# Encoder jobs of a hybrid transformer kernel: feed-forward, value products, norms and copies at other positions

## The reference

```python
x = x + encoder4(layernorm(x))   # 4 layers: 16 heads of 8, ALiBi + causal mask, FFN 128 -> 512 -> 128 with exact gelu, final norm
x = x + moe(layernorm(x))        # 8 experts, hyperbolic distances pick 2 of them per row
x = x + rope_attention(layernorm(x))
x = x + moe(layernorm(x))
```

## Time and profile before

| | us |
|---|---|
| median of 3 runs | 2651.41 (2651.28 to 2651.97) |
| profiled execution | 2659.2 |
| its span | 2657.4 |
| PE busy in the span | 2277.5 |
| DVE busy in the span | 1755.3 |
| ACT busy in the span | 1463.5 |

### The profile page before, as it was taken

The page is one execution under the profiler, slowest core; times in us unless marked ns, Lnnn a source line. Parts: engine busy times, 40 slices in busy tenths (PEclk is TensorE's granted clock), DMA queues, the critical chain, the costliest instruction groups (busy, mean ns, idle before and its releaser), DMA issues.

```text
span 2657.4 us, 102576 instructions
## 1 busy us (share of the span) xinstructions
PE 2277.5 (86%) x44398; PEld 1394.7 (52%) x44398; DVE 1755.3 (66%) x5525; ACT 1463.5 (55%) x2646; POOL 1037.8 (39%) x1261
## 2 busy tenths in 40 slices
PE   3689999999999999999998888996878778888983
PEld 1345555555555555555554444785644444436872
DVE  6877777777777777777877774422567777852212
ACT  0357677777677777777655556442245434454441
POOL 6334333333334333333444545423334554442135
PEclk9799999999999999999988988998888888889997
DMA  4253333342433333333222211575622222205773
GB/s 115 81 161 101 109 120 117 105 132 93 121 107 105 124 105 116 109 128 93 87 68 62 75 33 34 185 220 147 177 67 70 65 64 62 64 13 173 224 205 109
DMA packets 162531, 288.76 MB, mean 109 GB/s; under 512 B 28504, under 2 KB 116312, under 8 KB 160344
## 3 DMA queue, kind: packets, MB, share of 16 engines
q1 hardware_dynamic: 153696, 264.23, 33.0%
q0 software_dynamic: 8384, 17.97, 2.5%
HBM read 227.33 MB, written 95.96 MB: 122 GB/s over the span
## 4 chain that ended last, share of the span: by engine, by line
PE 61%; DVE 19%; ACT 7%; issue 4%; POOL 3%; SPq 2%; DMA 2%; another core or an unknown queue 2%; POOLq 0%; ACTq 0%; DVEq 0%
PE bank L481 23%; PE bank L647 9%; PE bank L601 9%; DVE mx L1281 6%; PE bank L787 5%; PE bank L797 5%; PE bank L665 3%; ACT big L878 3%; PE bank L488 2%; DVE xn L973 1%; DVE stats L960 1%; ACT OT L884 1%; PE bank L609 1%; ACT big L946 1%
## 5 line engine op out<-in xcount | busy, mean ns | idle before, releaser
L878 ACT ACTIVATE big<-bank 128x512 f32<-128x512 f32 x1600 | 919.8, 599 | 704.5 <-PE bank L481 662.5
L1281 DVE TENSOR_REDUCE mx<-bank 128x16 f32<-128x512 f32 (+1 forms) x1440 | 903.0, 654 | 417.1 <-PE bank L609 385.0
L1577 POOL TENSOR_SCALAR_AFFINE_SELECT big<-big 128x768 f32<-128x768 f32 (+1 forms) x640 | 392.9, 637 | 915.5 <-ACT big L878 915.1
L481 PE MATMUL bank<-QS,KS 99*32 99x512 bf16 (+3 forms) x10240 | 651.6, 312 | 46.1 <-ACT big L878 35.3
L601 PE MATMUL bank<-KS,QS 96*32 96x352 bf16 (+15 forms) x10240 | 592.5, 294 | 103.2 <-DVE mx L1281 63.4
L647 PE MATMUL bank<-big,V 128*9 128x512 f32 (+3 forms) x5120 | 457.8, 453 | 19.0 <-POOL big L1577 10.7
L601 PEld LDWEIGHTS bank<-KS,QS 96*32 96x32 bf16 x10240 | 243.1, 99 | 410.7 <-issue 177.3
L481 PEld LDWEIGHTS bank<-QS,KS 99*32 99x32 bf16 x10240 | 218.0, 99 | 220.4 <-ACT big L878 94.0
L609 PE MATMUL bank<-mask_a,ident_b 128*32 128x64 bf16 (+1 forms) x5760 | 305.8, 196 | 0.8 <-issue 0.5
L946 ACT ACTIVATE big<-bank,big 128x256 f32<-128x256 f32 x368 | 150.7, 471 | 253.4 <-PE bank L787 198.8
L647 PEld LDWEIGHTS bank<-big,V 128*9 128x9 f32 x5120 | 130.8, 92 | 154.7 <-issue 86.2
(11 more groups left out here) (216 smaller groups left out, 2727.4 us busy)
## 6 DMA issues: line engine op xcount, KB each, us to landing
big<-e_pack SPq DMA_DIRECT2D x92, 578.0 KB
QS<-part_scr SPq DMA_DIRECT2D x480, 96.0 KB
KS<-part_scr SPq DMA_DIRECT2D x480, 96.0 KB
part_scr<-parts SPq DMA_DIRECT2D x80, 384.0 KB
x_rows<-in_alibi SPq DMA_DIRECT2D x47, 384.0 KB, 4.9
y_rows<-in_alibi SPq DMA_DIRECT2D x47, 384.0 KB, 5.6
big<-x_rows SPq DMA_DIRECT2D x92, 128.0 KB
y_rows<-big SPq DMA_DIRECT2D x92, 128.0 KB
```

What stands on the lines that cost most here:

```text
L481: last = mm(out[c:c + 32], stationary[:, c:c + 32], moving, start=start, stop=stop)
L878: A(dst, src, ACT.Exp).then_inc(exp_done, 1)
L1281: v.tensor_reduce(mx[:, quad, k, 0:w], src, axis=AX.X, op=ALU.max).then_inc(a_used, 1)
L1577: g.affine_select(out=blocks, in_=blocks, compare_op=ALU.is_ge, fill=0.0, base=0, pattern=[[0, n], [1, P]], channel_multiplier=-1).then_in ...
```

## The change

Only positions change; no computation is added or left out. In encoder jobs the four positions without a maximum chunk are 13, 14, 22 and 38 instead of 9, 19, 29 and 39, so pass A of a job ends at position 29 instead of 28. The second feed-forward matrix goes in four pieces at positions 30, 30, 32 and 36. Rope jobs keep their positions. `TAIL_LEAD` is 6 instead of 5, and the late routing steps move by one position.

```diff
+WITHOUT = {False: (13, 14, 22, 38), True: (9, 19, 29, 39)}
-TAIL_LEAD, TAIL_RATE = 5, (2.0, 1.5)
+TAIL_LEAD, TAIL_RATE = 6, (2.0, 1.5)
 # PE, maximum chunks
-            quad, k = divmod(c, CPQ)
-            return (quad, k, APQ * quad + k) if k < APQ else (quad, None, None)
+            if (c - SKEW) % CHUNKS in WITHOUT[rope_job]:
+                return None, None, None
+            n = c - sum((pos + SKEW) % CHUNKS < c for pos in WITHOUT[rope_job])
+            return (*divmod(n, APQ), n)
 # PE
-                extras = [(xt, 2, (0, 1))]
+                extras = [(xt, 2, (0 if rope_job else 1, 1))]
-                    extras += [(lambda b, j, k=k: project(b, j, k), 2, (4 + 3 * k, 1)) for k in range(2)]
-                    extras += [(project_v, 2, (10, 1))]
+                    extras += [(lambda b, j, k=k: project(b, j, k), 2, (4 + 4 * k, 1)) for k in range(2)]
+                    extras += [(project_v, 2, (13, 1))]
-                    extras += [up_at(0, 26), up_at(1, 27), quad_at(1, (0,), 29), quad_at(1, (1,), 29),
-                               up_at(2, 29), up_at(3, 29), quad_at(1, (2, 3), 29)]
-                    extras += [(lambda b, j, t=t: ffn_down(b, j, t), -1, (29, 1)) for t in range(TT)]
+                KTS = ((0,), (1,), (2, 3))
+                if rope_job:
+                    quads = ((0, 0, (14, 18, 19)), (1, 0, (22, 23, 25)), (2, 0, (32, 33, 34)), (3, -1, (2, 3, 4)))
+                    sums = (7, 9, 11, 13)
+                else:
+                    quads = ((3, -1, (3, 5, 5)), (0, 0, (14, 19, 19)), (1, 0, (21, 29, 30)), (2, 0, (34, 38, 39)))
+                    sums = (7, 10, 12, 13)
+                if not rope_job:
+                    extras += [up_at(0, 28), up_at(1, 28), up_at(2, 29), up_at(3, 29)]
+                    extras += [down_at(0, 30), down_at(1, 30), down_at(2, 32), down_at(3, 36)]
-                extras += [(attn_transposes, -1, (15, 1)), (out_project, -1, (17, 1)), (max_transposes, 1, (31, 1))]
+                extras += [(attn_transposes, -1, (15 if rope_job else 16, 1)), (out_project, -1, (17 if rope_job else 18, 1)),
+                           (max_transposes, 1, (31 if rope_job else 33, 1))]
-                    extras += [(ffn_xt, -1, (24, 1))]
+                    extras += [(ffn_xt, -1, (25, 1))]
 # ACT: copy of xn 1 -> 2, of k 8 -> 9, sums of quads 0 to 2 20, 30, 36 -> 19, 31, 39, attention 15 -> 16
-                    extras += [(ffn_x, -1, (24, 1)), (ffn_gelu, -1, (27, 1))]
+                    extras += [(ffn_x, -1, (25, 1)), (ffn_gelu, -1, (27, 1))]
 # DVE
-                extras += [(add_x, -1, (18, 1)), (negate_split, 1, (28, 1)), (evac_max, 1, (31, 1)),
-                           (lns, 3, (33, 1)), (lna, 3, (36, 1))]
+                extras += [(add_x, -1, (18, 1)), (negate_split, 1, (28, 1) if rope_job else (30, 0)), (evac_max, 1, (31 if rope_job else 34, 1)),
+                           (lns, 3, (33 if rope_job else 25, 1)), (lna, 3, (36 if rope_job else 26, 1))]
-                    extras += [(ffn_lns, -1, (19, 1)), (ffn_lna, -1, (21, 1)), (ffn_add, -1, (30, 1))]
+                    extras += [(ffn_lns, -1, (19, 1)), (ffn_lna, -1, (21, 1)), (ffn_add, -1, (36, 1))]
 # POOL
-                          (lambda b, j: rsqrt(ln_index(b, j)), 3, (34, 1))]
+                          (lambda b, j: rsqrt(ln_index(b, j)), 3, (34 if rope_job else 26, 1))]
 # SP
-                          (lambda b, j: load(b, j, 1), 2, (20, 1)), (load_max, 1, (33 if rope_job else 32, 1)),
+                          (lambda b, j: load(b, j, 1), 2, (20, 1)), (load_max, 1, (33 if rope_job else 35, 1)),
```

More of the change, by code:

```diff
@@ L443, in spread_at @@
         def spread_at(n):
-            at = 23 if n == 0 else 24 + n if n <= 28 else 26 + n
+            at = 23 if n == 0 else 24 + n if n <= 28 else 27 + n
             return (-2 - at // CHUNKS, (at % CHUNKS, 1))
@@ L586, in pass_a @@
                 def pass_a(b, j, c):
-                    quad, k, n = a_chunk(c)
+                    quad, k, n = a_chunk(c, rope_job)
                     if k is None:
@@ L735, in attention @@
-                if not rope_job:
-                    extras += [up_at(0, 26), up_at(1, 27), quad_at(1, (0,), 29), quad_at(1, (1,), 29),
-                               up_at(2, 29), up_at(3, 29), quad_at(1, (2, 3), 29)]
-                    extras += [(lambda b, j, t=t: ffn_down(b, j, t), -1, (29, 1)) for t in range(TT)]
[L739 to L747, removed]
-                extras += [(attn_transposes, -1, (15, 1)), (out_project, -1, (17, 1)), (max_transposes, 1, (31, 1))]
+                def down_at(t, pos):
+                    return (lambda b, j: ffn_down(b, j, t), -1, (pos, 1))
@@ new lines, in quad_at @@
+                def quad_at(g, kts, rel, pos):
+                    return (lambda b, j: pv(b, j, g, kts), rel, (pos, 1))
+                KTS = ((0,), (1,), (2, 3))
[5 more added lines that the diff above has]
+                    sums = (7, 10, 12, 13)
@@ new lines, in attention @@
+                for g, rel, at in quads:
+                    extras += [quad_at(g, kts, rel, pos) for kts, pos in zip(KTS, at)]
+                if not rope_job:
+                    extras += [up_at(0, 28), up_at(1, 28), up_at(2, 29), up_at(3, 29)]
+                    extras += [down_at(0, 30), down_at(1, 30), down_at(2, 32), down_at(3, 36)]
+                extras += [(lambda b, j, t=t: ot_transposes(b, j, t), -1, (pos, 1)) for t, pos in enumerate(sums)]
+                extras += [(attn_transposes, -1, (15 if rope_job else 16, 1)), (out_project, -1, (17 if rope_job else 18, 1)),
+                           (max_transposes, 1, (31 if rope_job else 33, 1))]
@@ L755, in attention @@
                     route = ((route_transposes, 17), (route_project, 19), (route_dots, 22))
-                    extras += [(lambda b, j: route_ranks(j - ROUTE) if spread(j) else None, -3, (14, 1))]
+                    extras += [(lambda b, j: route_ranks(j - ROUTE) if spread(j) else None, -3, (15, 1))]
                     extras += [(lambda b, j, what=what: what(j - ROUTE) if j >= ROUTE else None, -2, (pos, 1))
@@ L888, in evac_attn @@
                     A(attnT[:], bankR[:], ACT.Copy).then_inc(attnT_ready, 1)
-                extras = [(xnt, 2, (1, 1))]
+                extras = [(xnt, 2, (1 if rope_job else 2, 1))]
                 if not rope_job:
[L892 to L896, removed]
+                    extras += [(lambda b, j, k=k: evac_qk(b, j, k), 2, (5 + 4 * k, 0)) for k in range(2)]
+                for g, rel, pos in ((3, -1, 5), (0, 0, 20 if rope_job else 19), (1, 0, 26 if rope_job else 31), (2, 0, 35 if rope_job else 39)):
+                    extras += [(lambda b, j, g=g: evac_ot(b, j, g), rel, (pos, 1))]
+                extras += [(evac_attn, -1, (15 if rope_job else 16, 1))]
                 def ffn_x(b, j):
@@ L1594, in attention @@
                     extras += [(lambda b, j: rsqrt(b + j, fln_step, frstd_ready), -1, (20, 1))]
-                    extras += [(lambda b, j, n=n: first_ln(b, j, n), 2, (17 + 8 * n, 1)) for n in range(2)]
+                    extras += [(lambda b, j, n=n: first_ln(b, j, n), 2, (17 + 6 * n, 1)) for n in range(2)]
                     route = ((lambda S: route_rsqrt(2 * S), -2, 1), (final_bias, -1, 33), (final_rows, -2, 4),
```

12 lines of the change are left out of this document (5 added, 7 removed).

## The result

The changed kernel takes 2708.89 us (median of 4 runs, 2706.53 to 2709.97); the kernel before, measured beside it, 2651.35 (2645.26 to 2651.97). The ratio is 1.0227, 95% interval 1.0207 to 1.0248: 57.5 us slower, where +36 were forecast and the range ended at 2704. The profiled execution took 2706.5 us, 47.3 more than that of before.

What follows compares the result with a forecast made beforehand. TensorE (PE), busy 86% of the span, was taken to bound the kernel, with its waits. 23 plain intervals x (0.7 waits + 0.9 clock) = +37 us on the median 2651.4 gave 2687 us, range 2625 to 2704.

Steps and rivals of the forecast that it cites:

- The main mechanism: Position 30's score chunk: PE waits 2.7 us a job for exp 28, its cover now standing behind the chunk.
- Chain on DVE: Output projection to second-layer transposes: the chain stays 6.0 us, PE has more work inside, gain 0.9 us a job.
- Load of the maxima: Position 0 of the next job: later copy and load make PE wait 0.5 us more, ends 0 and 1.5.
- DVE's wait for the power: Layer norm at 25 and 26: DVE waits about 0.7 us for POOL's square root; cost 0.2 us a job.
- The waits for maxima: PE's waits before the transposes and at positions 33 to 39 (0.67 us), expected to shrink or go.
- 45.7 + 0.7 = 46.4: Plain job without a clock fall: 45.7 us before, plus terms -0.9 + 2.7 - 1.8 + 0.2 + 0.5.
- other moves: Projections, head sums, attention transposes and positions without maximum chunk: 0 us a job, ends -0.4 and +0.4.
- The clock: PE's granted clock falls in 7 jobs of 10, 1.5 us each: +0.9 us a job, ends -0.2 and +1.3.
- The sum: 23 plain intervals x (0.7 + 0.9) = +37 us, routing jobs 0; added to median 2651.4, rounded down to 2687.
- The seven jobs with routing: Encoder jobs 25 to 31: 0 taken, as late DVE catches up in the wait; ends -20 and +15.
- Rival A: Faster: the 2.7 us wait overlaps with DVE lateness and DVE's relief stays; 2629 us, chance 0.27.
- Rival C: Worst: load of the maxima and layer norm at upper ends, a fall in every job; +2.6 x 23, 2711, chance 0.09.

Runs made afterwards that it cites:

- k2max_up: k2_max with the first up-projection at position 27 instead of 28; 2585.6 us, ratio 0.9773 to the kernel before.
- k2_slots: cover_k2 with the positions without a maximum chunk back at 9, 19, 29 and 39; 2632.1 us, ratio 0.9927 to the kernel before.
- k2_ln: cover_k2 with the layer norm back at 33 and 36 instead of 25 and 26, power on POOL at 34; 2685.1 us, ratio 1.0114.
- cover_k4: Changed kernel with the last value product and all four second-layer pieces at position 29; 2637.2 us, ratio 0.9952 to the kernel before.
- cover_k2: Changed kernel with the last value product and second-layer pieces 0 and 1 at 29, pieces 2 and 3 at 32 and 36; 2613.6 us, ratio 0.9859.
- after_max: Changed kernel with only the maxima's way earlier (transposes and copy at 32, load at 33), the wait for exp 28 left; 2689.3 us, ratio 1.017.
- k2_max: cover_k2 with the maxima's way earlier: transposes and DVE copy at 32, load on SP at 33; 2601.6 us, ratio 0.9809.
- before_apart: Kernel before with only the second-layer pieces at 30, 30, 32 and 36 instead of 29, the following addition at 36; 2678.6 us, ratio 1.0109.
- k2max_both: k2_max with the first up-projection at 27 and the pipeline-filling first layer norms moved earlier; 2584.7 us, ratio 0.9767 to the kernel before.
- cover_k: Changed kernel with only the last value product of quad 1 moved to position 29; 2654.7 us, ratio 1.0019 to the kernel before.

## Why the prediction was right and wrong

**The main mechanism was right, in place and size.** "PE waits 2.7 us in every job": 2.66 from start to start, 2.48 idle, 23 times in 23 jobs, released by exp 28. Chain on DVE: 5.75 us measured, 6.0 said. Load of the maxima: 0.45 us late, 0.5 said. DVE's wait for the power: 0.64 idle against 0.7. The waits for maxima are gone. A job without a fall takes 46.0 or 46.3, where 45.7 + 0.7 = 46.4 was worked out. Not costed was 0.29 us before the third up-projection, because the first gelu and its table load now start later with the first up-projection at 28; k2max_up later showed that this was worth 0.6 us a job.

**What took the waits for maxima away was put in the wrong place in part.** The longer one, ahead of the transposes, the prediction gave to the work that PE has more there, and said "6.0 us stay" for the chain; the free positions it put under "other moves", at 0 with ends of 0.4. With the free positions back (k2_slots) the stretch takes 6.7 us with a wait of 1.0 us in it, and the job is 1.1 us longer. The shorter one, between 33 and 39, it gave to the pieces at 32 and 36 and to the layer norm. It comes back neither with the layer norm back (k2_ln) nor with the pieces back (cover_k4) nor in k2_slots, so which move it was is open. All of these were tried on cover_k2 or beside it, with the wait at 30 gone, not in the changed kernel.

**The clock was mis-sized.** I took falls in 7 of 10 jobs; there were 21 in 23. In the 23 jobs, the two without a fall take 46.16 us on average and the 21 others 47.61, so a fall cost 1.45. Against the kernel before, the waits are +0.43 us a job (0.7 said) and the clock +1.13 (0.9 said), together 1.57 against the 1.6 stated. The total of the plain jobs, +36.0 against +37, is thus better than its two terms; that they made up for each other is luck. The sentence cited from the Trainium skill ("TensorE: Matmul & The Clock Gate", "HAM oscillation — how this bites in real kernels"), by which I let every job pay, came nearer than my 7 in 10. But that section tells of waits for a DMA of about 3 to 5 us, longer than any here, so it did not support the step to 2.7 us, and the runs go both ways: 21 of 23 jobs paid at 2.48 us idle in the changed kernel, 15 of 23 at the same 2.48 in after_max, none at 1.83. The drain that "ScalarE: Activation LUTs" of the Trainium skill ("What ACT_TABLE_LOAD costs") adds to a table load is again not in the trace: exp 28 starts 1.30 us after the load does.

**The step that failed is "The sum".** It counted 23 intervals and seven jobs with routing, and the start of the pipeline not at all. From 2687 to 2708.9 it is 21.9 us: 7.6 from the start of the pipeline, 1.2 from the jobs with routing, 2.6 from the rest, -1.0 from the plain jobs, 1.4 from rounding down, and 10.1 that lie between the profiled executions and the medians (below). Without the 7.6 us, or without the 10.1, the time would have been inside the range; it took both to pass 2704. The start, and PE's waits between 30 us and the first attention copy, the changed kernel first and then the kernel before:

```profile
0.00:220.20 220.20, 136.14 (x2906) 71.85 (x2910) 156.87 (x449) 76.62 (x131) 91.73 (x115) 0.87 0.39 112
0.00:212.60 212.60, 135.74 (x2894) 71.32 (x2896) 159.03 (x449) 75.97 (x130) 91.37 (x115) 0.90 0.41 116
```

```profile
PE bank L604 <- DVE mx L1287: 30.3, 20, 5.5
...
PE bank L604 <- DMA KS<-part_scr: 20.8, 2, 20.3
...
PE bank L484 <- DMA QS<-mT: 3.8, 2, 2.7
```

```profile
PE bank L601 <- DMA KS<-part_scr: 25.0, 2, 21.1
PE bank L601 <- DVE mx L1281: 18.4, 15, 4.1
...
PE bank L694 <- DVE mparts L1305: 4.6, 2, 2.3
```

PE is busy as long as before (136.1 and 135.7 us), so the 7.6 us are idle time and not work at a lower clock, though the clock is lower there (0.87, 0.90). PE waits 30.3 us for maxima where it waited 18.4, and for the load of the maxima 3.8 where it waited 4.6 for their parts; the wait for KS is 4.2 shorter. The start runs the same positions with DVE doing extra norms, so it fits that delays show there which a full job hides. The first attention copy comes at 162.2 instead of 154.6 us. With the maxima's way back alone (after_max) it comes at 158.6, with the layer norm back (k2_ln against cover_k2) 2.8 us earlier. These shares are rough. k2_max and k2max_up have the same program up to that copy, and it comes at 160.0 and 158.3; before_apart has that of the kernel before, and it comes at 155.7. And k2max_both has its first copy 6 us later than k2max_up (164.3) at the same median, so not every microsecond of the start is seen in the kernel's time.

**The seven jobs with routing** are nearly unchanged, +1.2 us, but not because nothing happens there: without the wait at 30 they take 391.4 us (cover_k2), 14 less than before the change. In the changed kernel the wait at 30 eats this up. The prediction took 0, between ends of -20 and +15.

**10 us are in no trace.** Profiled against profiled the difference is 47.3; the medians differ by 57.5. The profiled execution of before (2659.2) is 7.8 us above its median, that of the changed kernel (2706.5) 2.4 below, and 2659.2 lay above all 33 later runs of that kernel beside the experiments (2642.1 to 2656.5). So I stated the sum against a high draw and then against a median, with one value for both. What varies between executions of the same kernel by 14 us is open: their mean granted clocks go from 0.931 to 0.939, the higher ones mostly in the shorter executions.

**Rival A** (faster, because the waits overlap) was wrong as written: lateness of PE shifts both ends, and the wait is the same 2.48 us in every job. But its grounds, that DVE profits from pieces set apart, were right; cover_k2 against cover_k4 and the jobs with routing show that. **Rival C** has the nearest number, 2711, by luck: the load of the maxima and the layer norm were not at their upper ends (0.45 us late, and no wait of PE that the layer norm makes), and those ends with a fall in every job add up to +3.8 us a job, not to the 2.6 that it states.

## What to carry to other kernels

In an in-order program, what a block of work covers counts for more than where it balances the engines: before a block is spread, follow the longest chain it hides (here gelu, table load, exp) and leave in front of the consumer as many microseconds as the chain takes. A wait has a second price where it pulls the clock down, and that price can come at once: 0.65 us of cover were worth 2.2 us a job. Cost the fill of a pipeline by itself, ask of each moved item which queue it leaves alone as well as which it enters, and don't put a free position at nothing: here four of them were worth 1.1 us a job. State a forecast against the same kind of number that it is worked out from, a profiled execution or a median.

## What the runs showed of the hardware

The granted clock of PE reacts to single waits. With one wait of 2.48 us idle and 0.3 at each of three other places of the job it fell in 21 of 23 jobs; with the same wait and one of the 0.3 gone, in 15; with 1.83 us idle, in none (cover_k). In k2_ln waits of 1.90 to 2.26 us for a DMA brought falls in 16 of 23 jobs, so waits for a DMA do it as well as waits for an exp. The length of the wait is not all: in after_max every job has the same 2.48 us and a third stays up, and in k2_ln one wait of 1.91 us is followed by a fall and another is not. The falls come in a regular order, which shifts with the length of the job. A fall cost 1.45 to 1.7 us a job (changed kernel 1.45, before 1.5, after_max 1.65, k2_ln 1.7).
